# Grouping the output matmuls of attention by two pairs of key tiles, and splitting all expert weights in small chunks inside attention

## The reference

```python
q, k, v = heads(ln @ Wq.T), heads(kv[..., :INNER]), heads(kv[..., INNER:])
attn = softmax(where(full_mask, rmsnorm(q, qn_g) * SCALE @ rmsnorm(k, kn_g).T, -max))
x = x + (attn @ v) @ Wo.T + bo
z = layernorm(x)
weights, indices = top_k(softmax(z @ router_w.T), 2)      # 8 experts
h13 = z @ w13[e]; y_e = (silu(gate) * up) @ w2[e]         # w13[e]: 256 x 1024, w2[e]: 512 x 256
x = x + sum over the two experts of weight * y_e
```

## Time and profile before

| | us |
|---|---|
| time of three runs | 1182.6, 1184.58, 1185.38 (median 1184.58) |
| the profiled execution | 1183.16 |
| its span | 1181.3 |
| TensorE busy | 1000.8 (85%) |
| Pool busy | 698.9 (59%) |
| VectorE busy | 646.5 (55%) |
| ScalarE busy | 462.8 (39%) |

### The profile page before, as it was taken

One profiled execution on the slowest core, in us unless ns is written; L12 is line 12 of the kernel. 1 busy time (PEld: TensorE's weight loads), 2 busy tenths in 40 slices (PEclk: granted clock), 3 DMA queues, 4 the chain that ended last, 5 costly groups with the idle time before them and its releaser, 6 DMA issues.

```text
span 1181.3 us, 14830 instructions
## 1 busy us (share of the span) xinstructions
PE 1000.8 (85%) x4556; PEld 624.0 (53%) x4557; DVE 646.5 (55%) x1263; ACT 462.8 (39%) x667; POOL 698.9 (59%) x472
## 2 busy tenths in 40 slices
PE   2798506999999999999999999999972169999994
PEld 1565303454555555555555555555442158888884
DVE  3899607655555565555655556555128914444442
ACT  1455501444344544544544554454435013223331
POOL 4024440867787687677668767768756215565553
PEclk9899856999999999999999999999975559999998
DMA  6015550000000000000000000000063064333332
GB/s 184 1 47 185 186 187 22 1 1 1 1 1 1 14 14 1 14 14 2 13 14 5 10 14 14 1 14 14 5 240 143 0 260 124 51 51 50 53 53 27
DMA packets 38206, 59.95 MB, mean 51 GB/s; under 512 B 6827, under 2 KB 26220, under 8 KB 37132
## 3 DMA queue, kind: packets, MB, share of 16 engines
q1 hardware_dynamic: 24270, 42.40, 10.1%
q0 software_dynamic: 7488, 10.23, 5.4%
q10 hardware_dynamic: 6398, 6.69, 1.7%
HBM read 37.29 MB, written 22.02 MB: 50 GB/s over the span
## 4 chain that ended last, share of the span: by engine, by line
PE 73%; DVE 10%; DMA 9%; POOL 2%; issue 2%; ACTq 1%; ACT 1%; SPq 0%; DVEq 0%; POOLq 0%
PE bPV L1255 19%; PE bM L1175 12%; PE bS L1244 9%; PE bS L1245 9%; DMA wsp_d<-wraw 3%; DMA wraw<-w 3%; DVE mpart L877 2%; PE bG L1333 2%; PE bH L1350 1%; PE bY L1333 1%; PE bY L1335 1%; PE bY L1334 1%; PE bT L1190 1%; PE bG L1335 1%; PE bG L1334 1%
## 5 line engine op out<-in xcount | busy, mean ns | idle before, releaser
L877 DVE TENSOR_REDUCE mpart<-bM 128x1 f32<-128x464 f32 x492 | 305.0, 638 | 214.7 <-PE bM L1175 214.4
L441 POOL TENSOR_TENSOR acc_p<-acc_p,PT 128x1024 f32<-128x1024 f32 x160 | 381.2, 2382 | 66.8 <-ACT PT L656 60.5
L656 ACT ACTIVATE PT<-bS 128x1024 f32<-128x1024 f32 (+1 forms) x240 | 237.6, 997 | 321.3 <-PE bS L1245 319.4
L1255 PE MATMUL bPV<-PT,V 128*64 128x512 f32 x928 | 255.0, 617 | 0.0
L1175 PE MATMUL bM<-S,Q 128*128 128x464 f32 x492 | 198.3, 431 | 50.8 <-ACT Q L607 44.8
L1175 PEld LDWEIGHTS bM<-S,Q 128*128 128x128 f32 x492 | 93.4, 190 | 215.6 <-DVE mpart L877 151.3
L1244 PE MATMUL bS<-Q,S 128*128 128x512 f32 x464 | 186.7, 402 | 0.9 <-ACT Q L615 0.7
L1245 PE MATMUL bS<-Q,S 128*128 128x512 f32 x464 | 183.5, 395 | 0.0
L1244 PEld LDWEIGHTS bS<-Q,S 128*128 128x128 f32 x464 | 88.0, 190 | 34.6 <-issue 19.5
L1245 PEld LDWEIGHTS bS<-Q,S 128*128 128x128 f32 x464 | 87.7, 189 | 14.6
L447 POOL TENSOR_TENSOR acc_d<-acc_d,acc_p 128x1024 f32<-128x1024 f32 x16 | 38.0, 2373 | 87.3 <-DVE acc_d L909 87.3
(11 more groups left out here) (223 smaller groups left out, 1533.5 us busy)
## 6 DMA issues: line engine op xcount, KB each, us to landing
W<-wsp_d SPq DMA_DIRECT2D x8, 1536.0 KB, 8.2
wraw<-w SPq DMA_DIRECT2D x24, 256.0 KB, 2.9
wsp_d<-whi SPq DMA_DIRECT2D x24, 256.0 KB, 2.8
wsp_d<-wraw SPq DMA_DIRECT2D x24, 256.0 KB, 3.2
W<-w ACTq DMA_DIRECT2D x4, 1024.0 KB, 10.0
V<-x SPq DMA_DIRECT2D x1, 2048.0 KB, 12.8
W<-w ACTq DMA_DIRECT2D x4, 512.0 KB, 10.9
x<-x SPq DMA_DIRECT2D x12, 128.0 KB, 2.1
```

The source lines that it names most:

```text
L441: pool.tensor_tensor(acc_p[:], one, PT[:, q % NPT, :, :], ALU.add).then_inc(sem("z_p"), 1)
L656: act.activation(PT[:, p % NPT, 0:n, :], bS[(w.h + p) % 2][:, 0:n, :], ACT.Exp).then_inc(sem("exp"), 1)
L877: dve.tensor_reduce(mpart[:, i, g:g + 1], banks[k % len(banks)][:, 0:PIECE], AX, ALU.max)\
L1255: last = pe.matmul(bPV[b * D:(b + 1) * D, 0, :], V[:, c, h * D:(h + 1) * D], PT[:, p % NPT, b, :], start=c < 2, stop=c >= NK - 2, skip_gro ...
```

## The change

The constants: chunks of the split are 256 columns and all eight experts are split, 12 chunks each, six chunks (SHARE) in each unit. The blocks of Pool, ScalarE and SP that split weights before and after attention go, and the waits of VectorE for them. In attention ScalarE makes the high part (w_hi) after the exp of the pairs in SPLIT_AT, Pool the low part (w_lo) after the sums in LO_AT; `whi` is a single buffer, so w_hi waits for its store and for the low part before. SP keeps loading and storing chunks; the loads and stores of the finished tile move from SP to ScalarE. Pool has ten sums and VectorE three. Outputs come at odd pairs for two pairs together, and the last three pairs at the unit's end. After attention ScalarE loads both parts of experts 0 to 3 from `wsp_d`. Small buffers of the prologue and of attention now share their place. Left out below are allocations, and the removed blocks' bodies (the functions of the kernel before are printed above).

```diff
-WC = 512
+WC = 256
 NCH = EW // WC
-SC = 1024
-NSC = EW // SC
+SHARE = E * NCH // UNITS
...
-    wsp_d = nc.dram_tensor("wsp_d", [E - EARLY, 2, P, EW], F32, kind="Internal").ap()
+    wsp_d = nc.dram_tensor("wsp_d", [E, 2, P, EW], F32, kind="Internal").ap()
...
+        wraw = sb("wraw", [P, 2, WC], at=t1)
+        whi = sb("whi", [P, WC], F32R, at=t1)
...
             load(0)
             load(1)
-            for n in range(NSPL):
+            for n in range(E * NCH):
+                e, c = n // NCH, n % NCH * WC
+                sp.wait_ge(sem("whi"), n + 1)
+                sp.dma_start(wsp_d[e, 0, :, c:c + WC], whi[:].bitcast(F32)).then_inc(sem("wst_h"), 16)
                 sp.wait_ge(sem("wsplit"), n + 1)
-                e, c = n // NCH, n % NCH * WC
-                sp.dma_start(wsp_d[e, 0, :, c:c + WC], whi[:, n % 2, :].bitcast(F32)).then_inc(sem(f"wst{n % 2}"), 16)
                 sp.dma_start(wsp_d[e, 1, :, c:c + WC], wraw[:, n % 2, :]).then_inc(sem(f"wst{n % 2}"), 16)
-                sp.wait_ge(sem(f"wst{n % 2}"), 32 * (n // 2) + 32)
-                if n + 2 < NSPL:
+                if n + 2 < E * NCH:
+                    sp.wait_ge(sem(f"wst{n % 2}"), 16 * (n // 2) + 16)
                     load(n + 2)
...
-            sp.wait_ge(sem("w_in"), NSC * EARLY)
-            for e in range(EARLY, E):
+            for e in range(E):
                 sp.wait_ge(sem(f"we{e}"), 32)
-                sp.sem_inc(sem("w_in"), NSC)
+                sp.sem_inc(sem("w_in"), 1)
...
+            def w_lo(n):
+                pool.wait_ge(sem("whi"), n + 1)
+                pool.tensor_tensor(wraw[:, n % 2, :].bitcast(F32R), wraw[:, n % 2, :], whi[:].bitcast(F32),
+                                   ALU.subtract).then_inc(sem("wsplit"), 1)
+
             def unit(w):
                 for n in range(NZ):
                     z_sum(w, n)
+                    for k, at in enumerate(LO_AT):
+                        if n == at:
+                            w_lo(SHARE * w.u + k)
                     if n == XB_AT and w.fin:
...
+            def w_hi(n):
+                act.wait_ge(sem(f"raw{n % 2}"), 16 * (n // 2) + 16)
+                after(act, sem("wst_h"), 16 * n)
+                after(act, sem("wsplit"), n)
+                act.copy(whi[:], wraw[:, n % 2, :]).then_inc(sem("whi"), 1)
...
+            def x_load(t):
+                after(act, sem("ox"), 16 * t)
+                after(act, sem("x3"), t)
+                act.dma_start(x2[:], xt[t, :, :]).then_inc(sem("xin"), 16)
+
+            def x_store(t):
+                act.wait_ge(sem("x2"), t + 1)
+                act.dma_start(ot[t, :, :], x2[:]).then_inc(sem("ox"), 16)
+                act.wait_ge(sem("x3"), t + 1)
+                act.dma_start(xlt[t, :, :], x3[:]).then_inc(sem("ol"), 16)
...
                     if p == 0 and not w.last:
                         q_hi_1(v, w.next_h, w.next_b)
+                    if p == 1 and w.fin:
+                        x_load(w.tile)
+                    if p in SPLIT_AT:
+                        w_hi(SHARE * u + SPLIT_AT.index(p))
                     if p == HEADS_AT and w.h % 2 == 0 and not w.first:
                         heads_T(w)
...
                         act.copy(x3T[:], bT[:, 0, DIM:2 * DIM].rearrange("p (k c) -> p k c", k=2)).then_inc(sem("x3T"), 1)
+                        x_store(w.tile)
...
+            act.wait_ge(sem("wst_h"), 16 * E * NCH)
+            for k in range(2):
+                act.wait_ge(sem(f"wst{k}"), 16 * E * NCH // 2)
             for e in range(EARLY):
...
+                for half in range(2):
+                    act.dma_start(W[:, e, half, :].bitcast(F32), wsp_d[e, half, :, :]).then_inc(sem(f"we{e}"), 16)
...
                     pieces(p, 0)
-                    if p >= LAG:
-                        outputs(p - LAG)
+                    if p % 2 and p > 1:
+                        outputs(p - 3)
+                        outputs(p - 2)
                     pieces(p, 1)
...
-                for p in range(NP - LAG, NP):
+                for p in range(NP - 3, NP):
                     outputs(p)
...
-PIECES = ((0, 1), (2, 0)) + ((2, 1),) * 3 + ((1, 1), (2, 1), (1, 1), (2, 1)) + ((1, 1),) * 5 + ((0, 0),)
-OUT_AT, HEADS_AT, Y_AT, SD_AT, X3T_AT, LG_AT = 5, 7, 8, 9, 11, 12
+PIECES = ((1, 0), (2, 0)) + ((1, 0), (2, 2)) * 5 + ((2, 0), (2, 0), (0, 0))
+OUT_AT, HEADS_AT, Y_AT, SD_AT, X3_AT, X3T_AT, LG_AT = 5, 7, 8, 9, 10, 11, 12
 XB_AT = 2
-LAG = 2
-POOL_SUMS = ((0, 1),) + tuple((-1, p) for p in range(2, 12))
-DVE_SUMS = ((12, 13), (-1, 14))
+SPLIT_AT, LO_AT = (1, 3, 5, 7, 9, 11), (1, 3, 5, 7, 9, 9)
+POOL_SUMS = ((0, 1),) + tuple((-1, p) for p in range(2, 11))
+DVE_SUMS = ((11, 12), (-1, 13), (-1, 14))
```

More of the change, by code:

```diff
@@ L133, in build @@
         ident = sb("ident", [P, P])
+        small = ExitStack()
+        mcol = sb("mcol", [P, NK], at=small)
+        cols = sb("cols", [P, 8], at=small)
+        small.close()
+        twin = sb("twin", [P, D], at=small)
+        onec = sb("onec", [P, 1], at=small)
+        mpart = sb("mpart", [P, QB, NG], at=small)
+        cmax = sb("cmax", [P, QB], at=small)
+        orec = sb("orec", [P, QB], at=small)
+        st2 = sb("st2", [P, 6], at=small)
+        mv2 = sb("mv2", [P, 2], at=small)
+        sd2 = sb("sd2", [P, 1], at=small)
+        rs2 = sb("rs2", [P, 1], at=small)
+        small.close()
         wtab = sb("wtab", [P, NBLK])
@@ L139, in build @@
         ring_s = sb("ring_s", [P, 2], I32)
-        mcol = sb("mcol", [P, NK])
-        cols = sb("cols", [P, 8])
         eps = sb("eps", [P, 1])
@@ L192, in build @@
         rn = sb("rn", [P, 2 * H], at=t0)
-        wraw = sb("wraw", [P, 2, WC], at=t0)
-        whi = sb("whi", [P, 2, WC], F32R, at=t0)
         t0.close()
@@ L306, in _ @@
             sp.dma_start(rt[:], router_t.rearrange("(k p) n -> p k n", p=P)).then_inc(sem("c_rt"), 16)
+            sp.wait_ge(sem("klo"), NK)
+            sp.wait_ge(sem("s1"), NK)
+            sp.wait_ge(sem("qT"), NT)
             N13 = (DIM // P) * 2 * I // WC
             def load(n):
-                e, ch = EARLY + n // NCH, n % NCH
-                dst = wraw[:, n % 2, :]
+                e, ch = n // NCH, n % NCH
                 if ch < N13:
@@ L317, in load @@
                 else:
[L318 to L323, removed]
+                    src = w2[e, (ch - N13) * P:(ch - N13 + 1) * P, :]
+                sp.dma_start(wraw[:, n % 2, :], src).then_inc(sem(f"raw{n % 2}"), 16)
             load(0)
             load(1)
-            for n in range(NSPL):
+            for n in range(E * NCH):
+                e, c = n // NCH, n % NCH * WC
+                sp.wait_ge(sem("whi"), n + 1)
+                sp.dma_start(wsp_d[e, 0, :, c:c + WC], whi[:].bitcast(F32)).then_inc(sem("wst_h"), 16)
                 sp.wait_ge(sem("wsplit"), n + 1)
-                e, c = n // NCH, n % NCH * WC
-                sp.dma_start(wsp_d[e, 0, :, c:c + WC], whi[:, n % 2, :].bitcast(F32)).then_inc(sem(f"wst{n % 2}"), 16)
                 sp.dma_start(wsp_d[e, 1, :, c:c + WC], wraw[:, n % 2, :]).then_inc(sem(f"wst{n % 2}"), 16)
-                sp.wait_ge(sem(f"wst{n % 2}"), 32 * (n // 2) + 32)
-                if n + 2 < NSPL:
+                if n + 2 < E * NCH:
+                    sp.wait_ge(sem(f"wst{n % 2}"), 16 * (n // 2) + 16)
                     load(n + 2)
-            sp.wait_ge(sem("klo"), NK)
-            sp.wait_ge(sem("s1"), NK)
-            sp.wait_ge(sem("qT"), NT)
             xt = x.rearrange("(t p) d -> t p d", p=P)
@@ L342, in _ @@
             NF = NT - QB
[L344 to L352, removed]
             sp.wait_ge(sem("pv"), NP * UNITS)
@@ L374, in load_w @@
                 for half in range(2):
-                    sp.dma_start(W[:, e, half, :].bitcast(F32), wsp_d[e - EARLY, half, :, :]).then_inc(sem(f"we{e}"), 16)
+                    sp.dma_start(W[:, e, half, :].bitcast(F32), wsp_d[e, half, :, :]).then_inc(sem(f"we{e}"), 16)
             sp.wait_ge(sem("y_mm"), NT)
@@ L418, in _ @@
             run_steps(pool, 0, NC + 2, k_mask)
[L420 to L427, removed]
             NZ = len(POOL_SUMS)
@@ L476, in _ @@
             pool.memset(zrow[:], 0.0).then_inc(sem("zrow"), 1)
[L478 to L482, removed]
             pool.wait_ge(sem("routed"), 1)
@@ L642, in sd @@
                 act.activation(to, mv[:, 1:2], ACT.Sqrt, bias=eps[:, 0:1]).then_inc(sem("sd2"), 1)
+            def w_hi(n):
[3 more added lines that the diff above has]
+                act.copy(whi[:], wraw[:, n % 2, :]).then_inc(sem("whi"), 1)
+            xt = x.rearrange("(t p) d -> t p d", p=P)
+            ot = out[0:TOK, :].rearrange("(t p) d -> t p d", p=P)
+            xlt = xln_d.rearrange("(t p) d -> t p d", p=P)
+            def x_load(t):
[7 more added lines that the diff above has]
+                act.dma_start(xlt[t, :, :], x3[:]).then_inc(sem("ol"), 16)
             def unit(w):
@@ L695, in _ @@
             act.activation(ra[:], rb[:], ACT.Exp).then_inc(sem("r_ex"), 1)
```

(7 more changed lines are left out.)

5 lines of the change are left out of this document (removed).

## The result

The changed kernel takes **1140.52 us** (median of 4 runs, 1139.58 to 1143.53) against 1184.98 (median of 4, 1182.6 to 1185.9): a ratio of **0.9632**, 95% interval 0.9608 to 0.9656. Forecast were 1122 us and a range of 1078 to 1152. The span of the profiled execution is 1139.3 us.

What follows compares the result with a forecast made beforehand. Bounds: the hole before attention, TensorE in attention, the hole before the experts; afterwards the Pool to ScalarE chain. -45 - 23 - 3 + 2 - 10.8 + 13 + 5 = -62, so 1184.6 becomes 1122 us, range 1078 to 1152.

Steps and rivals of the forecast that it cites:

- The hole before attention: Before attention, VectorE's 40 us standing still until the split is stored goes; with faster small operations, -45 us.
- the small operations on 8 columns: Prologue, VectorE's L795: from 555 ns to about 190 ns without Pool's split; 5 us of the -45.
- routing: After attention: without Pool's 16 subtracts, 12 small VectorE operations take 3.0 instead of 26.0 us, -23 us.
- the mechanism in attention: Later units: ScalarE's copies wait for Pool's subtracts behind its sums, so x3T comes at 35.7 us and TensorE waits 4.4.
- The DMA loop: SP's chunk loads and stores in attention: 5.4 us just fits 5.6, nothing; rivals 5.8 us, +16 (12%), or 6.8, +96 (7%).
- the four x2t loads: Tail: x loads, 6.8 us to landing, now meet W's 12 KB rows; between 0 and +7, taken as +2 us.
- ScalarE's issues: Tail: ScalarE issues 8 loads at 0.52 us each instead of 8 us in all, so the last output's copy comes sooner, -3.
- The size of grouping: Attention on TensorE: seven fewer groups of outputs a unit, 0.38 us each, 2.7 us; -10.8 us for block 0's four units.
- Later units and last unit: Attention after block 0: 11 units of 43.5 instead of 42.37 us, +13, gain of grouping included; last unit +5.
- the coupling: Pool to ScalarE chain in later units, within the +13; rival that it is hidden: 1071 us, 15%; half hidden: 1096, 13%.
- the forecast's own sum of a unit: Later unit: x3T at 35.7 us, then routing to the unit's end 7.8 instead of 8.6, so 43.5 us.

Runs made afterwards that it cites:

- e3: The changed kernel with ScalarE's copies 1 to 5 one pair later (pairs 4, 6, 8, 10, 12): 1115.94 us, ratio 0.9405.
- e7: The changed kernel with Pool subtracting only 8 of each chunk's 256 columns, leaving out the rest of the low parts: 1109.19 us, ratio 0.9367.
- e4: The changed kernel with ScalarE's eight loads of W issued after the four x2t loads have landed: 1128.03 us, ratio 0.9507.
- e1: The kernel before with only the outputs grouped by two pairs and the pieces placed as in the change: 1159.52 us, ratio 0.9777.
- e2: The changed kernel without the grouping, outputs and pieces one pair at a time as before: 1172.74 us, ratio 0.9885.

## Why the prediction was right, and where it was off

*Right, and shown.* The hole before attention (-43.7), the small operations on 8 columns (172 ns, forecast 190), routing (-22.4), and the mechanism in attention: ScalarE's copy behind Pool's subtraction sets x3T (35.1 for 35.7 us), later units 43.9 on average (43.7 to 43.8 but for one) for 43.5, and TensorE idle before the transposes, projection and router. e3 and e7 take it away from two sides, the place of the wait and the work in it.

*The DMA loop.* ScalarE waited once for a store. 128 KB took 2.3 us for a load and 2.4 and 1.7 for the stores, by the DMA part of the page. The estimate from the Trainium skill's "DMA: Bandwidth & Descriptors", Anatomy of one DMA, 2.3 us, was met by two of the three (the section has its figures from DMAs that Pool issues, these were issued by SP); the loop was hidden all the same, so the 5.8 against 5.6 us did not decide, and no run here made it bind.

*The main miss: the tail.* The step was "the four x2t loads, 6.8 us to landing, now meet rows of 12 KB: between 0 and +7, I take +2", and "-3" for ScalarE's issues. The second was right, and hidden. Before, TensorE's transposes of the last unit waited for ScalarE's copy, which stood behind the issues, until 6.3 us after the last output, and VectorE's first x2t addition then waited for TensorE's projection, not for a load:

```profile
875.19 0.69 PE L1190 MATMUL bT<-twin,oT_a 128*128 128x64 f32 x2 [6.29 <-ACT oT_a L622]
...
883.56 0.42 DVE L914 TENSOR_TENSOR x2t<-x2t,bFY 128x256 f32<-128x256 f32 x1 [3.11 <-PE bFY L1202]
```

In the changed kernel the copy came at 843.13, 1.9 us behind the last output, and the transposes started at 2.7, when Pool's last sums were done. e4, where the x loads are out of the way, shows what that is worth: 11.0 us from the last output to the first x2t addition instead of 14.7: -3.6, where the forecast had -3. The other term failed. The loads landed after 14.1 us in the median, and the step asked who waits for one x load instead of the last: VectorE's copies of the iotas stand behind all four of Pool's additions. That cost +12.3 (23.4 for e4's 11.0) where the forecast had +2, or +7 at most; together +8.7 for -1. In the kernel before, the loads took 6.8 us too, but Pool's additions were done before TensorE's projection was, and cost nothing.

*The size of grouping.* "7 x 0.38 = 2.7 us, if nothing else binds. For the four units of block 0 nothing does": the switch was right (0.36), the "nothing" was not. 1.9 us came in each of the units 2 to 4 of block 0, in the changed kernel as in e1, and 1.6 in later ones (e1). The first unit of block 0 became only 1.4 shorter in the changed kernel, against 2.6 in e1 and e4 (38.76 us in both, 39.99 here), and that is the clock, not the grouping or the split: after a stand of 2.11 us TensorE's outputs at 169.39 ran at a granted clock of 0.53 (170.2 to 173.6). First the changed kernel, then e4, whose program is the same up to there and whose stand was 1.22 us:

```profile
169.39 2.71 PE L1250 MATMUL bPV<-PT,V 128*64 128x512 f32 x8
```

```profile
169.53 1.94 PE L1252 MATMUL bPV<-PT,V 128*64 128x512 f32 x8
```

So block 0's -7.0 is some -8.3 by grouping and the start of its first unit, and +1.2 by a clock that fell in this run.

*Later units and last unit.* +16.6 and +6.5 for +13 and +5. That the first came so near is partly luck. Two terms, both too large, had nearly cancelled: against e1's 448.77 the coupling costs 34 us, where the forecast had 43 (13 + 11 x 2.7), and grouping gives 17 for 30. In the forecast's own sum of a unit, the router's matmul came at 35.5 us for 35.7, and from there to the next unit's first score it took 8.3 for 7.8: grouping saves 0.3 there, not 0.8. One unit of 45.28 us (707.68 to 752.96) has the reduced clock as in e2 (0.96 granted over it), 1.5 us.

*Misses in sum.* 1.3 for the hole, 3.8 block 0, 3.6 later units, 1.5 last unit, 9.7 tail, 0.6 routing: 20.5, against 1140.5 - 1122 = 18.5 by the medians; the 2 us left are the profiled executions, of which the one before was 1.4 us below its median and the one after 0.7 above.

*Not settled.* What grouping gives less than its switches was read at one place (0.3 us), and not taken away. Doubling `whi`, a third way of freeing the copies, was not tried.

## What to carry to other kernels

When work is spread into a stage, give each added piece a place where its wait ends before the engine comes to it: moving five of six copies by one pair each (e3) was worth 24.6 us, over half of what the whole change gave. Price the chain and what stands behind its end on the next engine as a sum, not as a maximum. And ask of each load at a stage's end what is issued ahead of it on other queues, and who waits for the last of its kind, not for the first.

## What the hardware showed that I had not expected

Taking a wait away made another operation slower: VectorE's normalisation went from 0.41 us to between 1.54 and 1.92 (e3, 12 times) only because Pool, freed from its chain, was now in the middle of a sum. In the form that also writes a sum it takes 0.48 to 0.54.

TensorE's granted clock fell to its lower level for 3 to 6 us after stands of 1.93 us (e2, before 405.56) and 2.11 us (the changed kernel, before 168.98), and such units were 1.2 to 3.1 us longer than their like. But the length of the stand doesn't decide it here: in e2 it fell after one of 1.47 us (at 359.66) and stayed at 1.00 after one of 1.86 (at 498.21), in e1 it stayed after one of 2.00 (at 213.47), and the changed kernel's later units have stands of up to 1.54 us at 1.00. Two kernels that are the same up to there can differ by this (the first unit of block 0 in the changed kernel and in e4).

Small loads beside W's loads, whose rows have 12 KB, landed some 4 us apart and after 14.1 us in the median, instead of 2.2 us alone (e4). Changing from 128*128 matmuls to 128*64 ones and back costs 0.36 us each time here.
